# Expert stage of a one-core transformer kernel written out tile by tile: gathers ahead of the scatter-adds, the linear product two slots later

## The reference

```python
logits = jnp.dot(r_in, router_w)                      # [16, 256, 8]
probs = jax.nn.softmax(logits, axis=-1)
_, top_k_idx = jax.lax.top_k(logits, 2)
# weights of the two chosen experts, renormalised, times per_expert_scale
gate0 = jnp.einsum('bld,ehd->bleh', x, gating_w[:, 0])
gate1 = jnp.einsum('bld,ehd->bleh', x, gating_w[:, 1])
act = jax.nn.gelu(gate0) * gate1                      # hidden size 512
out = jnp.einsum('bleh,ehd,ble->bld', act, linear_w, combine)
x = x + tanh(g_ffn[1]) * out
```

## Time and profile before

| | us |
|---|---|
| median of 3 runs | 1825.58 |
| lowest, highest | 1823.18, 1827.15 |
| span of the profiled execution | 1821.2 |
| TensorE (PE) busy in the span | 1535.9 (84%) |
| DVE busy | 1215.9 (67%) |
| ACT busy | 926.7 (51%) |
| POOL busy | 593.8 (33%) |

### The profile page before, as it was taken

One profiled execution on the slowest core, in us unless ns is written; L12 is line 12 of the kernel. 1 busy time (PEld: TensorE's weight loads), 2 busy tenths in 40 slices (PEclk: granted clock), 3 DMA queues, 4 the chain that ended last, 5 costly groups with the idle time before them and its releaser, 6 DMA issues. The chain is left out here.

```text
span 1821.2 us, 39683 instructions
## 1 busy us (share of the span) xinstructions
PE 1535.9 (84%) x12540; PEld 1095.8 (60%) x12541; DVE 1215.9 (67%) x3316; ACT 926.7 (51%) x2530; POOL 593.8 (33%) x777
## 2 busy tenths in 40 slices
PE   3899999989989989998998999996628888888884
PEld 2667676676766767676675766765514544454452
DVE  6478888778887878878787887887433433334332
ACT  4477675666657657565665657666202222222221
POOL 3102323333232332423333232332332444444442
PEclk9899999999999999999999999998768999999997
DMA  8101202021020210203012020113006222222224
GB/s 236 58 2 59 70 2 71 13 61 65 7 72 3 69 45 29 70 2 72 13 59 66 7 71 2 52 48 111 30 16 207 45 42 46 43 43 46 41 45 119
DMA packets 78180, 98.39 MB, mean 54 GB/s; under 512 B 20576, under 2 KB 61680, under 8 KB 77936
## 3 DMA queue, kind: packets, MB, share of 16 engines
q1 hardware_dynamic: 51152, 77.01, 13.5%
q0 software_dynamic: 15872, 18.95, 6.5%
q10 hardware_dynamic: 10976, 0.13, 0.3%
HBM read 65.02 MB, written 35.23 MB: 55 GB/s over the span
## 5 line engine op out<-in xcount | busy, mean ns | idle before, releaser
L810 ACT ACTIVATE prob<-S,nm 128x256 f32<-128x256 f32 x512 | 235.5, 475 | 70.9 <-DVE nm L1506 67.6
L803 ACT ACTIVATE pTh<-T 128x512 f16<-128x512 f32 x256 | 139.3, 597 | 148.6 <-PE T L984 148.3
L1503 DVE TENSOR_REDUCE mx<-S 128x2 f32<-128x512 f32 x256 | 163.3, 679 | 39.9 <-PE S L1057 23.7
L1312 PE MATMUL S<-GL,xgh 128*128 x576 | 174.0, 384 | 10.6 <-issue 9.0
L654 POOL TENSOR_SCALAR ve_ln<-mv_ln 128x2 f32<-128x2 f32 x64 | 14.6, 228 | 484.6 <-DVE mv_ln L1477 484.1
L1515 DVE SCALAR_TENSOR_TENSOR pTl<-T,pTh 128x512 f16<-128x512 f32 x256 | 164.0, 681 | 3.4 <-ACT pTh L803 3.4
L819 ACT ACTIVATE prob<-prob,rden 128x256 f32<-128x256 f32 x256 | 116.3, 503 | 58.5 <-DVE p0n L1524 58.5
L725 POOL DMA_INDIRECT xg<-x_rows,trow x72 | 70.4, 977 | 228.2 <-DMA acc_rows<-ysb,yid 120.8
L984 PE MATMUL T<-ident,prob 128*128 128x128 f32 x1024 | 142.1, 283 | 1.5 <-DVE prob L1528 1.4
L979 PE MATMUL W<-cTh,Wkh 128*128 128x256 f16 x512 | 140.4, 274 | 0.0
L980 PE MATMUL W<-cTl,Wkh 128*128 128x256 f16 x512 | 140.4, 274 | 0.0
(11 more groups left out here) (296 smaller groups left out, 4534.9 us busy)
## 6 DMA issues: line engine op xcount, KB each, us to landing
cx<-in_ctx_dram SPq DMA_DIRECT2D x16, 512.0 KB, 5.4
gst<-in_L_ffn_gating_w_dram SPq DMA_DIRECT2D x16, 512.0 KB
gating_split<-gsp SPq DMA_DIRECT2D x16, 512.0 KB, 2.9
GL<-gating_split SPq DMA_DIRECT2D x8, 1024.0 KB, 5.2
stg<-in_L_xattn_Wkv_dram SPq DMA_DIRECT2D x8, 512.0 KB, 13.5
xl<-in_x_dram SPq DMA_DIRECT2D x16, 256.0 KB, 4.3
lst<-in_L_ffn_linear_w_dram SPq DMA_DIRECT2D x16, 256.0 KB
xres<-in_x_dram SPq DMA_DIRECT2D x16, 256.0 KB
```

What stands on the lines that cost most here:

```text
L803: A(flat(pTh[:, h, :, :]), T[h][:, :], ACT.Copy).then_inc(s_pTh[h], 1)
L810: ins = A(prob[:, h, t, :], S[h][:, t * NTOK:(t + 1) * NTOK], ACT.Exp, bias=nm[:, h, t:t + 1], scale=SM, accum_out=rs[:, h, t:t + 1])
L1312: ins = M(o[:, :], (xgl if n == 2 else xgh)[r % 2][:, k, :], GLflat[:, bass.ds(w, HID)], start=(k == 0 and n == 0), stop=(k == KD - 1 and ...
L1503: ins = V.tensor_reduce(mx[:, h, :], S[h][:, :].rearrange("p (t k) -> p t k", t=TT), AX.X, ALU.max)
```

## The change

The stage is written out tile by tile, without the hardware loop, so that every wait is for a constant and every buffer's number is fixed.

- N_TILES becomes (4096 x 2 + 8 x 127) // 128 = 71, the most that eight experts' lists can fill.
- The table rows of all tiles stay on chip in one buffer tab [128, 71, 2]. ACT loads them six tiles ahead (TABLE_AHEAD), with eight semaphores in turn. The copy yid goes: the scatter-add takes its token numbers from tab.
- There are 6 buffers ysb in place of 4; DVE waits for the landing of the scatter-add six tiles back before it writes one.
- POOL gathers three tiles ahead (GATHER_AHEAD), and the gather is issued before the wait for the previous scatter-add's landing.
- TensorE's order in slot i: first gating product of i, x_T of i+1, linear product of i-2, hidden_T of i-1, second gating product of i. DVE and ACT are put in the matching order.

The core of the diff (the same edits to the order on ACT and DVE, and the removed loop helper, are left out):

```diff
-N_TILES = NTOKENS * TOPK // P + E
+N_TILES = (NTOKENS * TOPK + E * (P - 1)) // P
...
+XG, YS, TB = 4, 6, 8
+GATHER_AHEAD, TABLE_AHEAD = 3, 6
...
-            def tile(i, quarter, r, front, back):
-                if isinstance(i, int) and i == 0:
-                    gather(0, 0, 0)
-                    gather(1, 0, 1)
-                wait_apart(pool, s_add, 16 * (i - 1))
-                if front and not (isinstance(i, int) and i + 2 >= N_TILES):
-                    gather(i + 2, quarter + (r % 4 + 2) // 4, (r + 2) % 4)
-                if back:
-                    b = (r - 1) % 4
-                    wait_apart(pool, s_yw, i)
-                    pool.indirect_dma_start(out=acc_d, out_offset=bass.IndirectOffsetOnAxis(ap=yid[b][:, :], axis=0),
-                                            in_=ysb[b][:, :], in_offset=None, compute_op=ALU.add)\
-                        .then_inc(s_add, 16)
...
+            for i in range(GATHER_AHEAD):
+                gather(i)
+            for i in range(N_TILES):
+                if i + GATHER_AHEAD < N_TILES:
+                    gather(i + GATHER_AHEAD)
+                at_least(pool, s_add, 16 * i)
+                pool.wait_ge(s_yw, i + 1)
+                pool.indirect_dma_start(out=acc_d, out_offset=bass.IndirectOffsetOnAxis(ap=tab[:, i, 0:1], axis=0),
+                                        in_=ysb[i % YS][:, :], in_offset=None, compute_op=ALU.add)\
+                    .then_inc(s_add, 16)
...
+            for i in range(TABLE_AHEAD):
+                table_in(i)
+            x_high(0)
...
+            x_T(0)
+            e_of = {0: expert(0)}
+            for i in range(N_TILES + 2):
+                if i < N_TILES:
+                    e = e_of[i]
+                    pe.wait_ge(s_we, e * 32 + 32)
+                    pe.wait_ge(s_xgl, i + 1)
+                    at_least(pe, s_gel, i)
+                    gate_half(i, 0, e * GL_SIZE, G0).then_inc(s_g0, 1)
+                if i + 1 < N_TILES:
+                    e_of[i + 1] = expert(i + 1)
+                    x_T(i + 1)
+                if i >= 2:
+                    linear(i - 2, e_of.pop(i - 2))
+                if 1 <= i <= N_TILES:
+                    hidden_T(i - 1)
+                if i < N_TILES:
+                    at_least(pe, s_act, i)
+                    gate_half(i, 1, e * GL_SIZE, G1).then_inc(s_g1, 1)
```

More of the change, by code:

```diff
@@ L334, in build @@
         GLflat = GL[:, :, :].rearrange("p a b -> p (a b)")
-        trow = [sb(f"trow{i}", [P, 2], I32) for i in range(4)]
-        xg = [sb(f"xg{i}", [P, D]) for i in range(4)]
+        tab = sb("tab", [P, N_TILES, 2], I32)
+        xg = [sb(f"xg{i}", [P, D]) for i in range(XG)]
         xgh = [sb(f"xgh{i}", [P, KD, P], FP16) for i in range(2)]
@@ L341, in build @@
         aH, aL = sb("aH", [P, HID], FP16), sb("aL", [P, HID], FP16)
-        ysb = [sb(f"ysb{i}", [P, D]) for i in range(4)]
-        yid = [sb(f"yid{i}", [P, 1], I32) for i in range(4)]
+        ysb = [sb(f"ysb{i}", [P, D]) for i in range(YS)]
         def pb(name):
@@ L489, in wait_apart @@
                 eng.wait_ge(sem, value)
[L491 to L500, removed]
         @block.sync
@@ L583, in _ @@
                 sp.wait_ge(s_scat[c], 16 * NB)
-            for r in range(3):
+            for r in range(GATHER_AHEAD):
                 sp.wait_ge(s_xg[r], 16)
@@ L962, in tile @@
                     A(aH[:, :], AP_[:, :], ACT.Copy).then_inc(s_ah, 1)
[L963 to L970, removed]
+                if i + TABLE_AHEAD < N_TILES:
+                    table_in(i + TABLE_AHEAD)
         @block.tensor
@@ L1324, in hidden_T, with linear @@
                 ins.then_inc(s_ap, 1)
[L1326 to L1337, removed]
+            def linear(i, e):
+                pe.wait_ge(s_al, i + 1)
+                at_least(pe, s_yw, i)
+                for c in range(4):
+                    for n in range(3):
+                        w = e * GL_SIZE + G_SIZE + ((c // 2) * 2 + (n == 1)) * 2 * D + (c % 2) * D
+                        ins = M(Y[:, 0:D], (aL if n == 2 else aH)[:, c * P:(c + 1) * P],
+                                GLflat[:, bass.ds(w, D)], start=(c == 0 and n == 0), stop=(c == 3 and n == 2))
+                ins.then_inc(s_lin, 1)
+            x_T(0)
[3 more added lines that the diff above has]
+                    e = e_of[i]
                     pe.wait_ge(s_we, e * 32 + 32)
@@ L1340, in tile @@
                     at_least(pe, s_gel, i)
[L1341 to L1344, removed]
-                    at_least(pe, s_act, i)
[L1346 to L1365, removed]
+                    gate_half(i, 0, e * GL_SIZE, G0).then_inc(s_g0, 1)
+                if i + 1 < N_TILES:
+                    e_of[i + 1] = expert(i + 1)
[4 more added lines that the diff above has]
+                    hidden_T(i - 1)
+                if i < N_TILES:
+                    at_least(pe, s_act, i)
+                    gate_half(i, 1, e * GL_SIZE, G1).then_inc(s_g1, 1)
         @block.vector
```

89 lines of the change are left out of this document (41 added, 48 removed).

## The result

| | before | with the change |
|---|---|---|
| median of 4 runs, us | 1826.05 | 1973.74 |
| lowest, highest | 1823.18, 1827.15 | 1967.19, 1983.11 |
| span of the profiled execution | 1821.2 | 1981.4 |

The ratio of the times is 1.0822, with a 95% interval of 1.0787 to 1.0856: slower by 148 us, where 111 were forecast. The profiled execution took 1983.11 us, the longest of the four; so what is read from its trace adds up to 160.2 us (1981.4 - 1821.2), not to 148.

The account below looks back on a forecast made before the run. A ring through POOL's queue and TensorE, closing once per tile, was to bind: 2.26 + 0.28 + 1.88 + 2.87 = 7.29 us, plus 0.38 for the clock, 7.67; with beginning and tail +111.0 us, 1937 us, range 1897 to 1985.

Parts of the forecast that it names:

- The ring as the bound: Expert stage: a dependency loop through POOL's queue and TensorE closes once per tile, 7.29 us before the clock, against 5.96 now.
- the 1.88 us from scatter-add to gather: On POOL, from the start of a scatter-add to the gather behind it: 1.58 us busy and 0.30 us of issue.
- Term 1: From the start of x_T (transposes of gathered rows) to the end of ysb (weighted rows), linear product between: 2.26 us.
- Term 4: From the start of a gather to the x_T that needs it: 2.87 us, of which 2.8 us is the landing.
- Term 2: From the end of ysb to the start of POOL's scatter-add: 0.28 us taken, 0.81 kept for the range.
- The clock: TensorE's idle time may drop its clock to 1.2 GHz: 1.51 us per slow tile, one in four taken, 0.38 us.
- The rival with every tile slow: TensorE at the low clock in every tile: 8.8 us a tile, time 2012 us; chance 0.08.
- The beginning: While the last five experts' weights load, gathers land in 5.0 us against 2.8; two to three rings, 6 us in all.
- The tail: The last three scatter-adds on POOL follow 4.59 us apart, 3 x 4.59 = 13.8 us.
- The start of the stage: First scatter-add at 1379.5 in place of 1379.08, behind one first gating product and one x_T more.
- the release costs 0.81 us here too: Rival: the scatter-add starts 0.81 us after ysb; 8.2 us a tile, 1972 us, within the forecast's range; no separate chance.
- The 4.4 us that I took for the time around the span: Median of the runs, 1825.58 us, lies 4.4 above the profiled span of 1821.2; taken as unchanged time around the span.

Follow-up runs that it names:

- the version with four ahead: The changed kernel with gathers issued four tiles ahead in place of three and five buffers xg: 1723.48 us, ratio 0.9449 to the kernel before.
- the exchanged waits: The changed kernel with POOL's two waits ahead of the scatter-add in the other order, ysb first, then the previous landing: 1939.55 us.
- the filled version: The changed kernel with ten unused 512-column matmuls behind each first gating product from tile 2 on, filling TensorE's idle time: 1947.70 us.
- the version with late loads: The changed kernel with SyncE's five loads of expert weights held back until eight tiles are scaled: 1975.81 us, ratio 1.0847 to the kernel before.

## Why the prediction was right in sign and short in size

- **The ring as the bound: right.** "Three tiles ahead, minus the two slots, leave one slot" held, and the version with four ahead shows that nothing else made the kernel slow. The order of POOL, the vanished wait for the landing, the waits of TensorE and DVE and the 1.88 us from scatter-add to gather (1.89) are all in the trace.
- **Term 1, x_T to the end of ysb: 2.26, measured 2.26. Term 4, gather to x_T: 2.87, measured 2.77 and 2.87 in the two rings shown.**
- **Term 2, the release, is the step that failed: 0.28 taken, 0.81 measured.** It is 67 x 0.53 = 35.5 us of the miss, and the exchanged waits gave 34.2 us back. I took the difference in the earlier trace rows for one between a constant and a register; it is one of which wait comes last. The first scatter-add has a single wait (ysb ends at 1383.65, it starts at 1383.93), all later ones have two, in the loop as in the written-out code. The rows of the change's own order on POOL showed it: one wait at the first scatter-add, two at the next.
- **The clock: 0.38 a tile taken, (8.27 - 7.82) = 0.45 measured** (7.82 is the forecast's 7.29 with the release at 0.81; the filled version's rings measured 7.81), 29 us in this execution against 25.5; the filled version gives 26.0 between medians. The price of a slow tile, 1.51 us, came out: 9.3 us rings beside 7.8. How many there would be was a choice between two bounds, so that one in four came near is partly luck: 13 rings of 65 have the whole price and 12 a part of it. The prediction had the reason why not all are slow, a shorter idle time behind a slow tile (1.65 us above), but didn't draw from it that slow and fast tiles would alternate. The idle time ahead of a slow tile is 2.96 to 3.13 us in the rows shown and not 2.5, since the release lengthens it too. TensorE is therefore busy 63 to 70 us of 100, not 61: the low clock makes the same work longer. The rival with every tile slow did not come. The Trainium skill (TensorE: Matmul & The Clock Gate, section on HAM oscillation) has a kernel that restarts slow in every tile; here the trace shows it in part of the tiles only.
- **The beginning: 6 us taken, 11.7 measured** (13.41 + 13.97 - 2 x 7.82). The landing of 5.0 us in the earlier trace rows is the median of five gathers; the two on which these rings wait reached x_T after 6.90 and 7.50 us, 8.7 us more than twice 2.87. The other 3.0 us are the low clock in both tiles, 1.5 us each, which the forecast counted only in the steady rings.
- **The tail: 3 x 4.59 = 13.8 taken, 13.67 measured, by luck.** The three steps are 5.67, 4.09 and 3.91 us. The first still waits for ysb; the other two wait for the landing, whose wait the DMA itself carries here, and are 0.5 to 0.7 us shorter than in the loop. With the waits exchanged the same two are 4.57 and 4.43 us. What follows the tail is unchanged.
- **The start of the stage: 1379.5 forecast, 1383.93 in the profile.** Of this, 4.8 us arose before the stage: POOL's first write to the routing table is at 1354.98 in place of 1350.16. In the version with late loads the first scatter-add is at 1378.45, so it is this execution's own.

The sum for the profiled execution: 4.4 + 35.5 + 3.5 + 5.7 = 49.1 us above the forecast of 1913.2 for the last scatter-add, which is at 1962.29. Between medians the miss is 36.7 us (1973.74 - 1937), about the size of the release alone (the profiled execution was 9 us longer than the median); the rival "the release costs 0.81 us here too" had 1972 us. The 4.4 us that I took for the time around the span were not that either: in all four runs of the change the time is 1.7 to 1.8 us above the span.

## What to carry to other kernels

Count the lead of a prefetch in slots between the transfer's place in its queue and its use, less the slots by which the work ahead of it in that queue was postponed; divide the latency around the ring by that number and compare it with the busiest engine. Work that is postponed by a slot takes a tile of lead from every transfer that stands behind it: here one number in the source, three or four, was worth 250 us. And leave the second-nearest bound some room, for late transfers are caught up only where the step can be shorter than the mean. Where an engine waits for two events ahead of a DMA, write the one that comes last first.

## What the runs showed of the hardware that was not expected

- An indirect DMA on POOL starts 0.28 to 0.29 us behind the event it waits for when that wait is its only one or the first written of two, and 0.81 us when it is the second, which POOL's sequencer executes by itself. For a landing in place of ysb the two are 0.27 us (four tiles ahead) and 0.79 us (the same with the waits exchanged). The Trainium skill (Perfetto Trace Analysis, section on identifying dependency chains) says that an instruction with several waits may have separate semaphore instructions ahead of it; the trace agrees, and adds the price of 0.5 us here.
- A gather of 128 rows lands in 2.8 us, but reaches its user after 6.9 and 7.5 us (5.6 to 6.3 with the loads moved) while 1.5 MB per expert are being loaded on another queue.
- Idle times of 3.10 and 2.96 us of TensorE, one tile apart, ended at 2.4 GHz in the first case and at 1.2 GHz, some way into the product, in the second. The idle time alone doesn't tell which; a kernel near this should be costed between both. A slow tile shortens the idle time behind it (1.65 us after 3.08), and in this trace no slow tile is followed by another slow one.
